# Attention's values products: both heads of a pair in one instruction, in two halves of the query tiles

## What is computed

```python
    q = (x @ wq).reshape(b, s, H, NOPE + ROPE)
    ...
    scores = jnp.einsum('bqhd,bkhd->bhqk', qf, k) * scale
    causal = jnp.tril(jnp.ones((s, s), dtype=bool))
    scores = jnp.where(causal[None, None], scores, jnp.float32(-1e+30))
    attn = jax.nn.softmax(scores, axis=-1)
    o = jnp.einsum('bhqk,bkhd->bqhd', attn, v).reshape(b, s, H * VD)
    return o @ wo
```

## Time and profile before

| | |
|---|---|
| Median of 3 runs | 1423.64 us (1423.6 to 1424.46) |
| The profiled execution, its own time | 1421.54 us |
| Its span, first to last instruction | 1419.7 us |
| TensorE busy | 1357.7 us, 96% |
| VectorE / ScalarE / GpSimd busy | 60% / 47% / 27% |
| Mean granted TensorE clock | 0.985 of full speed |
| Attention | about 212 us to 978 us of the span |

### The profile page before, as it was taken

The page is one execution under the profiler, slowest core; times in us unless marked ns, Lnnn a source line. Parts: engine busy times, 40 slices in busy tenths (PEclk is TensorE's granted clock), DMA queues, the critical chain, the costliest instruction groups (busy, mean ns, idle before and its releaser), DMA issues. The chain is left out here.

```text
span 1419.7 us, 23230 instructions
## 1 busy us (share of the span) xinstructions
PE 1357.7 (96%) x7092; PEld 1140.3 (80%) x7092; DVE 858.7 (60%) x1761; ACT 670.4 (47%) x1551; POOL 381.8 (27%) x339
## 2 busy tenths in 40 slices
PE   6899998999999999999999999998998999989997
PEld 3666777888888888888888888886776888868885
DVE  5786754655666666666776566665574434434568
ACT  3333326666666666666666666662312223222232
POOL 0334453000003091030640123700042233322262
PEclk9999999999999999999999999998998999999998
DMA  9999877966677669685799766874635789887374
GB/s 294 374 388 339 299 282 270 361 202 228 200 269 266 224 226 321 207 318 196 269 365 368 244 225 196 295 292 174 248 127 200 280 304 331 304 329 258 128 241 136
DMA packets 160042, 375.59 MB, mean 265 GB/s; under 512 B 23144, under 2 KB 80556, under 8 KB 147680
## 3 DMA queue, kind: packets, MB, share of 16 engines
q1 hardware_dynamic: 144432, 314.34, 63.1%
q0 software_dynamic: 15536, 60.30, 11.9%
HBM read 245.84 MB, written 128.22 MB: 263 GB/s over the span
## 5 line engine op out<-in xcount | busy, mean ns | idle before, releaser
L1155 ACT ACTIVATE a_pr<-a_pr,a_stat 128x128 f32<-128x128 f32 (+3 forms) x256 | 142.0, 556 | 113.8 <-DVE a_stat L1226 113.5
L1326 PEld LDWEIGHTS a_psY<-a_pT,a_cv 128*128 128x128 f32 x768 | 124.9, 190 | 15.9 <-issue 2.1
L1226 DVE CUSTOM_DVE_ANT_0 a_pr<-a_psS,f_mask 128x128 f32<-128x128 f32 (+3 forms) x256 | 114.6, 487 | 31.4 <-PE a_psS L1314 31.0
L1326 PE MATMUL a_psY<-a_pT,a_cv 128*128 128x512 f32 (+3 forms) x768 | 131.2, 320 | 1.9 <-DVE a_pT L1245 1.9
L1161 ACT ACTIVATE a_pr<-a_pr,a_stat 128x128 f32<-128x128 f32 (+3 forms) x256 | 122.2, 548 | 0.0
L1171 ACT ACTIVATE a_oT<-a_psY 128x512 fp32r<-128x512 f32 x64 | 38.2, 598 | 151.0 <-PE a_psY L1326 151.0
L1256 DVE TENSOR_TENSOR n_acc<-a_psZ,n_acc 128x512 f32<-128x512 f32 x125 | 86.4, 691 | 35.2 <-PE a_psZ L104 33.0
L1240 DVE TENSOR_TENSOR a_oT<-a_psY,a_oT 128x512 fp32r<-128x512 f32 x64 | 44.2, 691 | 103.7 <-ACT a_oT L1171 103.7
L102 PE MATMUL a_psX<-a_hT,a_wqk 128*128 128x512 f32 (+1 forms) x256 | 100.3, 392 | 0.6 <-DVEq L1216 0.6
L103 PE MATMUL a_psX<-a_hT,a_wqk 128*128 128x512 f32 (+1 forms) x256 | 100.4, 392 | 0.0
L104 PE MATMUL a_psX<-a_hT,a_wqk 128*128 128x512 f32 (+1 forms) x256 | 100.1, 391 | 0.0
(11 more groups left out here) (354 smaller groups left out, 3469.6 us busy)
## 6 DMA issues: line engine op xcount, KB each, us to landing
w1s_d<-a_ws SPq DMA_DIRECT2D x72, 512.0 KB, 3.5
a_wqk<-wqk_d SPq DMA_DIRECT2D x64, 512.0 KB, 4.6
a_mh<-mhl_d SPq DMA_DIRECT2D x32, 1024.0 KB, 6.2
s_ring<-w1s_d SPq DMA_DIRECT2D x16, 2048.0 KB, 9.4
w2s_d<-a_ws SPq DMA_DIRECT2D x72, 256.0 KB, 4.0
qpe_d<-p_qs SPq DMA_DIRECT2D x16, 1024.0 KB, 5.1
a_rw<-in_L_ffn_rw SPq DMA_DIRECT2D x128, 128.0 KB, 3.5
a_qpe<-qpe_d SPq DMA_DIRECT2D x64, 256.0 KB, 2.7
```

What stands on the lines that cost most here:

```text
L1155: nc.scalar.activation(pr[i], pr[i], ACT.Exp, bias=nmax[:, i:i + 1], scale=-1.0, accum_out=rsum[:, i:i + 1]).then_inc(ex, 1)
L1226: nc.vector.tensor_tensor_reduce(out=pr[i], in0=score[i][:, 0:w], in1=mask[:, S - w:S], scale=-1.0, scalar=3e38, op0=ALU.add, op1=ALU.min, ...
L1326: m = nc.tensor.matmul(psY[:, q0:S], cv[:, j, cs], pT[:, ps, o:o + w], start=n == 0, stop=n == 11)
```

## The change

The values product is no longer made per head but per pair, for both heads at once, in two halves of the query tiles. A matmul now streams a piece of the one head and the same piece of the other (`pT` holds both), and writes two pieces of `psY`, whose left half belongs to one head and whose right half to the other. Half 0 is query tiles 0 and 1: three matmuls of 2x256 columns (key tile 0) and three of 2x128 (key tile 1). Half 1 is query tiles 2 and 3: nine matmuls of 2x256 and three of 2x128. That is 18 matmuls for a pair, where there were 24.

The order changes with it. Both halves of pair n-1 run in the first turn of pair n: half 0 right behind the scores, half 1 where the values were. The output tiles of pair n-1 all run in the two turns of pair n: tile 0 in the first, tiles 1, 2 and 3 in the second, the last of them into `psY`. Handing over to ScalarE and VectorE (`o_high`, `o_low`) happens twice in the first turn and not at all in the second. The core of the diff:

```diff
-        pT = sb("a_pT", [P, 2, NPT], F32R)
+        pT = sb("a_pT", [P, 2, 2, NPT], F32R)
...
-        oT = sb("a_oT", [P, 4, 2, S], F32R)
+        oT = sb("a_oT", [P, 2, 2, S], F32R)
...
+        HALF_ = [(slice(0, 2 * P), [(0, 0, 2), (1, 0, 1)]), (slice(2 * P, S), [(0, 2, 2), (1, 1, 2), (2, 0, 2), (3, 0, 1)])]
+        ends = [psS[:, 2], psZ[:, :]]
+        rest = [(B * PAIRS - 2, 3)] + [(B * PAIRS - 1, t) for t in range(TB)]
+        two_of = lambda bank: bank.rearrange("p (u n) -> p u n", u=2)
... (ScalarE)
                         exps(g)
+                        if not u and early:
+                            if early == 1:
+                                A.stored(act)
+                            o_high(n - 1, 0)
                         split_high(*todo[0])
                         shares(g)
                         if not (last and u):
                             q_high(g + 1)
...
-                        if u:
-                            if not early:
-                                A.stored(act)
-                            o_high(g - 1, n, v * 2, early < 2)
-                        elif early:
-                            o_high(g - 1, n - 1, 3 - v * 2, early < 3)
-                        p_high(g)
+                        if not u and early:
+                            o_high(n - 1, 1)
+                        p_high(g, u)
... (VectorE)
+                        first = u and early
+                        softmax(g, lambda: add_out(n - 1, 1) if first else None)
+                        if early and not u:
+                            o_low(n - 1, 0)
                         split_low(*todo[0])
+                        if early and not u:
+                            add_out(n - 1, 0)
                         if not (last and u):
                             q_low(g + 1)
-                        out(1)
+                        if first:
+                            add_out(n - 1, 2)
...
-                        if u or early:
-                            o_low(g - 1, v * 2 if u else 3 - v * 2)
-                        p_low(g)
+                        if first and not last:
+                            add_out(n - 1, 3, psY[:, :])
+                        if early and not u:
+                            o_low(n - 1, 1)
+                        p_low(g, u)
... (TensorE)
-                def values(g):
-                    pe.wait_ge(landed_c, g // H + 1)
-                    pe.wait_ge(p_lo, g * 3 + 4)
-                    pe.wait_ge(o_lo, g + 1)
...
+                def values(n, half, bank=psY[:, :], ahead=0):
+                    pe.wait_ge(landed_c, n // PAIRS + 1)
+                    pe.wait_ge(p_lo, n * 6 + 7)
+                    if half == 0:
+                        pe.wait_ge(ac, n * 4 + TB - ahead)
+                    elif ahead == 0:
+                        pe.wait_ge(o_lo, n * 2 + 2)
+                    parts = [(j, i, k, cs, ps) for j, i, k in HALF_[half][1] for cs, ps in ((0, 0), (0, 1), (1, 0))]
+                    for m, (j, i, k, cs, ps) in enumerate(parts):
+                        o = OFF[j] + i * P
+                        last = nc.tensor.matmul(two_of(bank)[:, :, (2 - k) * P:2 * P], cv[:, j, cs],
+                                                pT[:, :, ps, o:o + k * P], start=m == 0, stop=m == len(parts) - 1)
+                    last.then_inc(pv, 1)
...
                         scores(g, u)
-                        out(0)
+                        if early:
+                            if u:
+                                output(n - 1, 1 - v, 1)
+                            else:
+                                values(n - 1, 0)
                         if not (last and u):
                             qproj(g + 1, 1 - u, g)
-                        out(1)
-                        if u or early:
-                            values(g - 1)
+                        if early:
+                            if u:
+                                output(n - 1, 1 - v, 2)
+                                if not last:
+                                    output(n - 1, 1 - v, 3, psY[:, :], 1)
+                            else:
+                                output(n - 1, 1 - v, 0)
+                                values(n - 1, 1)
...
-                values(B * H - 1)
                 for i, (n, t) in enumerate(rest):
-                    output(n, n % 2, t, ends[i % 2], 1 if i else 0)
+                    output(n, n % 2, t, ends[i % 2], 1)
+                    if i == 0:
+                        values(B * PAIRS - 1, 0, ahead=1)
+                        values(B * PAIRS - 1, 1, psX[:, :], 1)
```

More of the change, by code:

```diff
@@ L973, in stage_attention @@
                   (psX[:, 0:2 * P], slice(OFF[2], OFF[2] + 2 * P), [(2, 0)])]
-        ends = [psZ[:, :], psS[:, 2]]
-        rest = [(B * PAIRS - 2, 2), (B * PAIRS - 2, 3)] + [(B * PAIRS - 1, t) for t in range(TB)]
+        HALF_ = [(slice(0, 2 * P), [(0, 0, 2), (1, 0, 1)]), (slice(2 * P, S), [(0, 2, 2), (1, 1, 2), (2, 0, 2), (3, 0, 1)])]
+        ends = [psS[:, 2], psZ[:, :]]
+        rest = [(B * PAIRS - 2, 3)] + [(B * PAIRS - 1, t) for t in range(TB)]
+        two_of = lambda bank: bank.rearrange("p (u n) -> p u n", u=2)
         DBL = (10, 12)
@@ L1165, in q_high, with o_high, p_high @@
                     nc.scalar.activation(qT[:, 0], psX[:, :], ACT.Copy, scale=SCALE).then_inc(q_hi, 1)
-                def o_high(g, n, s, fresh):
-                    act.wait_ge(pv, g + 1)
-                    if not fresh:
-                        act.wait_ge(ot, n * 4 - 3)
-                    nc.scalar.activation(oT[:, s, 0], psY[:, :], ACT.Copy).then_inc(o_hi, 1)
-                def p_high(g):
+                def o_high(n, half, bank=psY[:, :]):
+                    act.wait_ge(pv, n * 2 + half + 1)
+                    nc.scalar.activation(oT[:, :, 0, HALF_[half][0]], two_of(bank), ACT.Copy).then_inc(o_hi, 1)
+                def p_high(g, u):
                     for k, (src, dst, _) in enumerate(groups):
                         act.wait_ge(pt, g * 3 + k + 1)
-                        nc.scalar.activation(pT[:, 0, dst], src, ACT.Copy).then_inc(p_hi, 1)
+                        nc.scalar.activation(pT[:, u, 0, dst], src, ACT.Copy).then_inc(p_hi, 1)
                 def split_high(b, i):
@@ L1207, in _ @@
                 run(act, pair)
-                o_high(B * H - 1, B * PAIRS - 1, 3, False)
+                for half in range(2):
+                    o_high(B * PAIRS - 1, half, (psY if half == 0 else psX)[:, :])
             @block.vector
@@ L1282, in _ @@
                 run(dve, pair, True)
-                o_low(B * H - 1, 3)
+                add_out(*rest[0], ends[0])
+                for half in range(2):
+                    o_low(B * PAIRS - 1, half, (psY if half == 0 else psX)[:, :])
                 for i, (n, t) in enumerate(rest):
+                    if i == 0:
+                        continue
                     add_out(n, t, ends[i % 2])
@@ L1314, in scores @@
                         nc.tensor.matmul(out, qpe[:, u, q], k_(kpe, 1), start=False, stop=True).then_inc(sc, 1)
-                def values(g):
-                    pe.wait_ge(landed_c, g // H + 1)
-                    pe.wait_ge(p_lo, g * 3 + 4)
-                    pe.wait_ge(o_lo, g + 1)
-                    n = 0
-                    for j in range(TB):
-                        q0 = j * P
-                        o = OFF[j]
-                        w = S - q0
-                        for cs, ps in ((0, 0), (0, 1), (1, 0)):
-                            m = nc.tensor.matmul(psY[:, q0:S], cv[:, j, cs], pT[:, ps, o:o + w], start=n == 0, stop=n == 11)
-                            n += 1
-                    m.then_inc(pv, 1)
+                def values(n, half, bank=psY[:, :], ahead=0):
[11 more added lines that the diff above has]
+                    last.then_inc(pv, 1)
                 def transposes(g):
@@ L1350, in pair @@
                         g = n * 2 + u
-                        if u:
-                            out = (lambda t: output(n - 1, 1 - v, t)) if early else (lambda t: None)
-                        else:
-                            out = (lambda t: output(n - 2, v, 2 + t)) if early > 1 else (lambda t: None)
                         scores(g, u)
-                        out(0)
+                        if early:
[3 more added lines that the diff above has]
+                                values(n - 1, 0)
                         if not (last and u):
                             qproj(g + 1, 1 - u, g)
-                        out(1)
-                        if u or early:
-                            values(g - 1)
+                        if early:
[6 more added lines that the diff above has]
+                                values(n - 1, 1)
                         if not (last and u):
```

22 lines of the change are left out of this document (10 added, 12 removed).

## The result

| | before | changed |
|---|---|---|
| median of 8 runs, us | 1423.8 (1418.05 to 1426.56) | 1432.03 (1428.78 to 1436.61) |
| ratio | | 1.0061 (95%: 1.004 to 1.0081) |
| profiled execution, us | 1421.54 | 1432.7 |
| last matmul of the output tiles starts at | 976.36 | 983.10 |

The forecast was 1417.1, in a range of 1412.5 to 1421.5. The kernel became 8.2 us slower instead of 6.5 faster.

A forecast was written before the change was run, and what follows sets the result against it. TensorE was taken as the bound, the attention lasting as long as its instruction starts; -7.3 + 1.5 + 0.5 + 1.3 + 1.1 - 4.0 = -6.9, with +0.4 gives -6.5 from 1423.64: 1417.1 us, range 1412.5 to 1421.5.

The forecast's parts named there:

- pairs: Values matmuls in ordinary turns: 0.25 us gained a pair over 29 whole pairs, -7.3 us (-6.7 to -8.1).
- output tile behind the statistics: After row statistics, late exponentials make output tile 0 wait about 0.5 us at three places, +1.5 us.
- heads 44 to 46: Turns that split two weights: ScalarE waits for raw weights, so TensorE's gain of two pairs is lost, +0.5 us.
- start, turns and clock: First heads: values leave head 1's turn and later turns fill up, +1.3; a 3 us gap likely lowers the clock, +1.1.
- end: Last pair: an output tile fills the wait for the shares, and fewer output tiles follow the values; -4.0 us.
- VectorE's splits beside GpSimd: VectorE's weight splits slow where GpSimd works; with a possible clock fall at the end, +0.4 us for both.
- edges: In the narrow-matmul rival, what remains outside the pairs' gain: -0.8 us, with +0.4 and +0.4 added.
- Do the waits stay hidden?: Step checking a pair's turns: half 0, output tile 0 (0.58 us cover) and queries' low part all come in time.
- two pieces cost like two matmuls: Rival on the values matmuls: 0.3 us more a pair, +9.3 in 31 pairs, 1433 us; chance 0.07.
- a narrow matmul costs its columns only: Rival on the values matmuls: gain only 0.03 us a pair, time 1423.6 us; chance 0.06.
- the handover of half 0 is late: Rival in every first turn: low part 0.3 us beyond its cover costs 9.3 us, half landing at 1420 to 1424; chance 0.12.
- predicted waits for `a_oT`: Sign of being right: waits before output tile 0 in the turns of heads 24, 40 and 56 and nowhere else.

The follow-up runs named there:

- e1: On the changed kernel, GpSimd multiplies and clears `acc` before its waits for the landing of the next loads; 1419.73 us, 0.9974 to before.
- e4: On the changed kernel, output tiles one place later (0, 1, 2 in the next pair's second turn, 3 in the turn after); 1418.28 us, 0.9968 to before.
- e5: On the changed kernel, VectorE does the next queries' low part ahead of the addition of output tile 0; 1420.16 us, 0.9979 to before.
- e3: On the kernel before, three needless memsets on GpSimd ahead of its multiplication of `acc` at each sequence change; 1441.1 us, 1.0133 to before.
- e2: On the kernel before, GpSimd's multiplication and clearing of `acc` moved ahead of its landing waits; 1424.99 us, 1.0014 to before.
- e7: On the changed kernel with `acc` taken first, VectorE's row statistics moved from the turn's end to behind the split weight; 1430.26 us, 1.0046 to before.
- e8: Like the early-statistics kernel, but VectorE's last small statistics instruction, which releases GpSimd, is back at the turn's end; 1416.48 us, 0.9956 to before.
- e6: On the kernel with output tiles one place later, 12 needless matmuls ahead of the transposes of heads 0 and 1; 1414.58 us, 0.9939 to before.
- e9: On the kernel with later output tiles and needless matmuls at the start, ten more before head 45's transposes; 1413.18 us, 0.9922 to before.

## Why the prediction was wrong

Its terms beside the two profiled executions, in us:

| term of the sum | predicted | measured | from |
|---|---|---|---|
| pairs | -7.3 | -7.5 | 29 x (23.07 - 23.33) |
| output tile behind the statistics | +1.5 | +1.0 | turns 24, 40, 56 against 11.91 |
| heads 44 to 46 | +0.5 | +0.4 | excess over ordinary turns, 3.05 against 2.67 |
| start, turns and clock | +2.4 | +3.0 | turns 1 to 3, 36.40 against 33.41 |
| end | -4.0 | -3.8 | turn 62, turn 63 and what follows, 32.53 against 36.30 |
| change of sequence | 0 | +13.7 | turns 18, 19, 34, 35 |

With -0.3 before the first transposes these make 6.5, and the last matmul of the output tiles starts 6.7 us later.

The prediction added +0.4 for VectorE's splits beside GpSimd and for a fall of the clock at the end. Nothing answers to it: ordinary turns have no wait, and the clock is whole from head 63's transposes to 983.10. One figure of the rivals is added up wrong: 15 ns a pair, with the same edges as in the sentence before it (+0.4 and +0.4), gives 1424.0 and not 1423.5.

**The step that failed** is "Do the waits stay hidden?", and in it the sentence "So the ordinary turn runs without a wait, and 29 whole pairs". It followed the chains of half 0, of output tile 0 and of the queries' low part, and put the addition of tile 0 ahead of that low part, "which ends about 9.3". It asked of this addition only when its product is there. For one tile in 32 the addition has a second condition, that GpSimd has cleared `acc`, and the change brings it forward by most of a turn. The trace of before held the answer: the clearing ends at 441.89, the addition starts at 441.99, and the change has VectorE ready for it at 434.44, 7.5 us earlier. No rival held it, and the range didn't reach it. e1, e4 and e5 each take one link out of the chain (the release, the position of the tile, the position of the addition) and gain 12.3, 13.8 and 11.9 us; with the link restored in the old kernel (e3) the stall is there without the change. e2 shows that the move of e1 has no value of its own.

**What held.** The gain of a pair, 0.26 for 0.25, with 11.91 + 11.16 for the predicted 11.90 + 11.19. The two pieces cost nothing: the mean distance from start to start of two values matmuls of the same width is 232.9 ns for 512 columns and 118.2 for 256, against 232.5 and 118.4 before. The groups by shape, changed kernel (there an instruction's busy time overlaps the next one's):

```profile
L1337 PE MATMUL a_psY<-a_pT,a_cv 128*128 128x512 f32 x375 | 97.6, 395 | 0.3 <-issue 0.3
...
L1337 PE MATMUL a_psY<-a_pT,a_cv 128*128 128x256 f32 x189 | 32.7, 281 | 0.0
```

With these steps "two pieces cost like two matmuls" falls, with the gain of 0.26 for its 0.03 "a narrow matmul costs its columns only", and "the handover of half 0 is late" too: in ordinary turns TensorE has no idle time. Of the predicted waits for `a_oT` the list holds one, 0.2 us at head 24, but all three are there: the first matmul of output tile 0 starts 0.61, 0.27 and 0.50 us behind the queries' last at heads 24, 40 and 56, for an ordinary 0.23, and the second 0.1 later than usual behind the first. e4, e7 and e8, where these turns are 11.91, show that it comes from the statistics. The start was mis-sized by 0.6, by its term for the clock: turn 2 is 13.67 for an ordinary 11.91, so 1.8 for the 1.1 predicted (e6 gives 1.7). The wait before head 1's transposes is 2.81 where 3 was said. At the end, the changed kernel behind the last transposes, which answers to the earlier trace rows:

```profile
971.26 1.09 PE L1346 MATMUL a_psT<-ident,a_pr 128*128 128x128 f32 x8 [0.52 <-ACT a_pr L1163]
...
974.30 1.29 PE L1337 MATMUL a_psY<-a_pT,a_cv 128*128 128x512 f32 x6 [0.34 <-issue]
975.42 2.61 PE L1337 MATMUL a_psX<-a_pT,a_cv 128*128 128x512 f32 x12
...
983.10 0.39 PE L104 MATMUL a_psS<-a_mh,a_oT 128*128 128x512 f32 x1
```

From 971.26 to 983.10 it is 11.84, for the predicted 11.9. Had the change of sequence been what it was before, the same sum with the measured terms gives -7.2 for the forecast's -6.5; e1, which removes it, has 0.9974 to before, or -3.7 us (-6.1 to -1.1), so some of it doesn't show even there. In its profile the last matmul of the output tiles starts 4.5 us earlier than before (971.87); it has 1.6 us more than the changed kernel in turn 46 and 1.3 more in turn 2, where the clock was down for 3.4 us (not at all in the changed kernel) and for 6.8 (3.4 there).

**What stays open.** The stage behind the attention has the same 1992 matmuls in both kernels, and took over 4 us more in this execution. The windows, before and changed:

```profile
977.00:1419.70 442.70, 413.96 (x1992) 340.47 (x1992) 233.33 (x424) 121.97 (x263) 126.80 (x146) 0.97 0.67 242
```

```profile
984.00:1430.90 446.90, 417.76 (x1992) 342.97 (x1992) 232.86 (x424) 121.71 (x263) 125.79 (x146) 0.96 0.67 239
```

Measured from the end of the last output matmul to the end of the span, it took 443.0 us (before) to 450.2 in the eleven profiles, 447.4 in the changed kernel; the 450.2 are e2's, whose attention is as long as before. The clock was at one half for 24.6 us of it before, 31.4 with the change and 34.1 in e2. So it isn't put down to the change, and what sets the clock there in one execution or another wasn't tried.

## What to carry to other kernels

When a consumer moves earlier in a list, look up each of its waits and not only that for its data: conditions that hold once in many rounds, such as a buffer handed back by another engine, have to be compared time against time in the trace of before, and a consumer that starts at a fixed short distance behind such an event (here 0.10 us, three times of three) is already waiting for it, whatever releaser its row names. Then go down the releasing engine's list and see whether it could do its part earlier: here two landing waits that concerned something else cost 13.7 us, and moving the multiplication and the clearing ahead of them took them away. And a short stall of TensorE has a second price in its clock, which needless matmuls in the gap can save if the gap ends with something else anyway.

## What was not expected of the hardware

VectorE's split of a weight, which reads two tiles of SBUF, took 0.96 us alone and 6.60 us in e7, where it started 0.8 us ahead of a group of four GpSimd additions, at 514.26, and ended at 520.86, 0.83 behind the end of the whole group (520.03). In the changed kernel at 432.57, 0.23 into another such group, it took 1.87 and so got through after the first of four; in the kernel before one that started in the third of four, at 711.10, took 2.99. The Trainium skill, page "SBUF — State Buffer", section "SBUF: two separate sides", has the two engines share a pair of ports as an exclusive lock, for a VectorE instruction with two SBUF inputs, held for the whole instruction by the one that starts first. The row at 432.57 agrees, with GpSimd's instruction ahead of it. The one of e7 doesn't: VectorE's started first and was held up all the same, past one GpSimd instruction after another. e7 has this twice, at 514.26 and 895.08, 6.60 us both times, and both started 0.13 or 0.14 us into GpSimd's issue of a transfer right ahead of its additions. No other split did that: those that started in such an issue with nothing behind it took 0.96, and those that started among the additions 1.3 to 3.7. That this is what decides isn't shown.

In the changed kernel's attention the clock fell to one half, 1.2 GHz, five times, each time in a wait of TensorE or up to 1.6 us behind it. The waits were 1.7, 2.7 and 2.8 us at the start, 4.2 and 4.3 at the changes of sequence. The length alone doesn't decide: behind 2.4 us at 763.18 it didn't fall, nor behind 3.0 at 518.62 in e7. It was down for 3.4 us at each of the falls at the start (from 218.44, 228.68 and 238.92 on) and for 6.8 us at the changes of sequence (440.31, 631.45). What this adds to the waits is 2.7 and 2.2 us in the turns of heads 19 and 35, 3.2 us in the first two turns (e6 against e4), and 1.6 us in turn 46 (e9 against e6); the latter two are what filling the gap with matmuls brought back.
